# A two-layer graph network on one core: node states and destination rows kept in SBUF instead of DRAM, and a reordered end

## The reference

```python
h = relu(layernorm(x))                      # layer 0: GATv2
xl, xr = h @ Wl + bl, h @ Wr + br
m = leaky_relu(xl[src] + xr[dst] + edge_weight1 @ We, 0.2)
p = softmax of (m @ att) over the edges of each dst
g = gelu(h + segment_sum(xl[src] * p, dst) + bias_out)
x = x + batchnorm(g) * bn_gamma + bn_beta
h = relu(layernorm(x))                      # layer 1: gated messages
em = relu(layernorm(concat(h[src], h[dst]) @ msg_w + msg_b)) * edge_weight
messages = segment_sum(em, dst) / counts
gate = sigmoid(h @ gate_w + gate_b)
u = relu(layernorm(concat(h, messages) @ upd_w + upd_b, upd_g, upd_beta))
x = x + gate * u + (1 - gate) * h
```

## Time and profile before

| | |
|---|---|
| median of 3 runs | 2326.95 us (2321.8 to 2328.92) |
| the profiled execution | 2325.57 us, span 2323.7 us |
| busy share of the span | PE 69%, PEld 50%, DVE 66%, ACT 44%, POOL 71% |
| granted TensorE clock, mean of the span | 0.921 of full speed |
| DMA | 233.58 MB in 222657 packets, mean 101 GB/s |
| costliest group | L697, GpSimd's gathers: 1638 of them, 1573.8 us busy, mean 961 ns |

### The profile page before, as it was taken

The page is one execution under the profiler, slowest core; times in us unless marked ns, Lnnn a source line. Parts: engine busy times, 40 slices in busy tenths (PEclk is TensorE's granted clock), DMA queues, the critical chain, the costliest instruction groups (busy, mean ns, idle before and its releaser), DMA issues.

```text
span 2323.7 us, 45075 instructions
## 1 busy us (share of the span) xinstructions
PE 1608.6 (69%) x10064; PEld 1151.3 (50%) x10064; DVE 1539.4 (66%) x5042; ACT 1027.0 (44%) x3827; POOL 1646.2 (71%) x1729
## 2 busy tenths in 40 slices
PE   5588787777777777777676776656566656656564
PEld 4366454555545555555465554444444444445443
DVE  6667665656565555655568886776666667676757
ACT  4444443444444444434454554444444444444435
POOL 5677777777777777777037777777777777777753
PEclk9799999999999999999778898998989899898997
DMA  8633333333333333333652343333333333333324
GB/s 222 181 99 98 96 96 88 96 89 95 88 96 92 93 95 88 95 88 77 158 166 70 98 106 96 87 95 87 95 87 94 91 91 86 93 96 88 93 63 111
DMA packets 222657, 233.58 MB, mean 101 GB/s; under 512 B 116266, under 2 KB 166332, under 8 KB 222533
## 3 DMA queue, kind: packets, MB, share of 16 engines
q0 software_dynamic: 55168, 114.83, 20.1%
q1 hardware_dynamic: 165958, 117.37, 18.8%
q10 hardware_dynamic: 1472, 0.73, 0.2%
HBM read 196.29 MB, written 36.46 MB: 100 GB/s over the span
## 4 chain that ended last, share of the span: by engine, by line
POOL 53%; issue 20%; PE 11%; DVE 7%; DMA 6%; ACT 1%; POOLq 1%; SPq 1%; DVEq 0%; ACTq 0%
POOL room L697 53%; DMA room<-src_table,rec 3%; PE psum L951 2%; PE psum L878 2%; PE psum L956 1%; PE psum L969 1%; DMA dst_table<-rows 1%; PE psum L778 1%; PE psum L860 1%; PE psum L850 1%; PE psum L843 1%; DMA room<-state 1%; DVE stats L1352 1%; DVE rows L1364 0%; PE psum L868 0%
## 5 line engine op out<-in xcount | busy, mean ns | idle before, releaser
L697 POOL DMA_INDIRECT room<-src_table,rec x1638 | 1573.8, 961 | 523.8 <-issue 486.1
L951 PE MATMUL psum<-room,ident 128*128 128x384 f32 (+1 forms) x512 | 273.1, 619 | 370.5 <-DMA room<-src_table,rec 313.9
L1242 ACT ACTIVATE room<-psum 128x128 f32<-128x128 f32 x832 | 219.0, 274 | 541.4 <-DVE room L1778 538.8
L1592 DVE TENSOR_TENSOR room<-psum,room 128x384 f32<-128x384 f32 (+1 forms) x256 | 151.2, 591 | 386.9 <-ACT room L1174 216.3
L1174 ACT ACTIVATE room<-psum 128x384 f32<-128x384 f32 (+1 forms) x256 | 131.8, 515 | 523.2 <-PE psum L850 516.9
L1778 DVE TENSOR_TENSOR room<-psum,msg_g 128x384 f32<-128x384 f32 (+1 forms) x256 | 151.0, 590 | 275.9 <-PE psum L956 267.6
L951 PEld LDWEIGHTS psum<-room,ident 128*128 128x128 f32 x512 | 85.7, 210 | 404.0 <-issue 363.7
L969 PE MATMUL psum<-room 128*125 128x128 f32 x1664 | 264.4, 302 | 1.6 <-ACT room L1254 1.6
L878 PE MATMUL psum<-room 128*125 128x128 f32 x1664 | 254.0, 293 | 16.5 <-ACT room L1192 10.6
L956 PEld LDWEIGHTS psum<-room 125*128 125x128 bf16 x2496 | 185.9, 108 | 129.5 <-issue 107.5
L1792 DVE SCALAR_TENSOR_TENSOR room<-room,rstd_e,msg_beta 128x128 f32<-128x128 f32 x832 | 242.5, 349 | 10.2
(11 more groups left out here) (224 smaller groups left out, 2228.6 us busy)
## 6 DMA issues: line engine op xcount, KB each, us to landing
room<-dst_perm SPq DMA_DIRECT2D x128, 416.0 KB
room<-src_table,rec POOLq DMA_INDIRECT x1638
room<-dst_table SPq DMA_DIRECT2D x128, 64.0 KB
src_table<-rows SPq DMA_DIRECT2D x24, 224.0 KB
dst_table<-rows SPq DMA_DIRECT2D x24, 224.0 KB
st_in<-state SPq DMA_DIRECT2D x64, 65.5 KB
st_in<-state SPq DMA_DIRECT2D x64, 64.0 KB
state<-st_out SPq DMA_DIRECT2D x64, 64.0 KB
```

Of the source, the lines that this page charges most:

```text
L697: pool.indirect_dma_start(out=xg[:, u, t * P:(t + 1) * P], out_offset=None, in_=table[:, :], in_offset=bass.IndirectOffsetOnAxis(ap=rec[:, ...
L951: nc.tensor.matmul(msg_bank[b][:, cols], ident[:, :], xg[:, u, t0 * P:t1 * P], start=True, stop=False, skip_group_check=True)
L1242: i = nc.scalar.activation(sq[:, j * P:(j + 1) * P], msg_bank[b][:, j * P:(j + 1) * P], ACT.Square, accum_out=var_e[:, c, j:j + 1])
```

## The change

Every state stays in SBUF. `held` is [125 partitions, 52 tiles, 128], `held_den`, `held_max` and `cnt` hold sum, maximum and count, and `dst_rows` holds the destination rows; all are filled where they are made, and nothing of them passes through DRAM. For this the layout is turned: node n is on partition n % 125, in tile n // 125. A window of 125 nodes that starts anywhere then lies on all 125 partitions, in two neighbouring tiles: partitions from `left` up belong to tile `start`, those below to `start` + 1. The pair's entry in `pair_list` holds chunk, `start`, `base` and `left`. VectorE reads `start` into a register twice per pair (`start_of`), makes two columns `side` (1 where the partition belongs to the first or the second tile), picks the window's rows (`pick_rows`), and merges into both tiles, with factors that are neutral where `side` is 0. SyncE's window, state and factor loads and the state stores are gone; the load of the pair's entry now waits for the state of pair k-2. The masks of layer 0 are bf16 instead of f32. `feat_h` and `held` share one room, which is zeroed by GpSimd in two fills behind the projections and by VectorE before the second loop.

Between the loops, TensorE turns `node_h` in place of the product with `feat_h`. At the end, the update weights and bias are centred over the features ahead of time, so that the product's rows have mean zero: the statistics then are a sum of squares by ScalarE (`squares_out`). The product `upd_beta` x gate is made for 10 groups by GpSimd and 3 groups by ScalarE, to be added by VectorE: `weighted` (one pass per group), `gated` (one per tile), `added` (one per group). `OUT_PARTS` has five parts. `GB_ACT` is (10, 11, 12).

The core of the diff, with the indent cut by 8; most of the removed lines are left out, since they stand above:

```diff
+feat_room = sb("feat_room", [P, NC * D])
+feat_h = feat_room[:, 0:NT * PP].rearrange("p (t n) -> p t n", n=PP)
+held = feat_room[0:PP, :].rearrange("p (t f) -> p t f", f=D)
+dst_rows = sb("dst_rows", [PP, NC, D])
+cnt = sb("cnt", [PP, NC])
+held_den = sb("held_den", [PP, NC])
+held_max = sb("held_max", [PP, NC])
...
-nmask = take(2 * CH).rearrange("p (u e) -> p u e", u=2)
+nmask = take(CH).bitcast(BF16).rearrange("p (u e) -> p u e", u=2)
...
-    return table[0:N, :].rearrange("(p t) f -> p t f", t=NT)[p0:p1, t0:t1, :]
+    return table[0:N, :].rearrange("(t p) f -> p t f", p=PP)[p0:p1, t0:t1, :]
...
+            if not there(k, -2, end):
+                return
+            two, three = two_chunks(k + 2)
...
+            sp.wait_ge(s.oh, k + 1)
+            settle(sp)
+            if n == 0:
+                sp.wait_ge(s.mask, nth(k + 1, 0))
                 settle(sp)
-                sp.wait_ge(s.split, k + 1)
+            load_dst(s, v, two)
+            if n == 0:
...
+                load_ew(two, v)
+            ge(sp, s.state, k - 1)
+            settle(sp)
+            load_info(s, k + 2, (u + 2) % U)
+        all_pairs(sp, slot, last, 0)
...
+    done = 10 * GT * PP
+    pool.wait_ge(s_proj, 10)
+    pool.memset(feat_room[:, 0:done], 0.0).then_inc(s_zero, 1)
+    pool.wait_ge(s_proj, NG)
+    pool.memset(feat_room[:, done:NC * D], 0.0).then_inc(s_zero, 1)
...
-    for g in RELU_POOL:
-        pool.wait_ge(s_ub, g + 1)
+    pool.wait_ge(s_gate, NG)
+    pool.wait_ge(msg.win, last + U)
+    for g in GB_POOL:
         for t in range(*GROUPS[g]):
-            i = pool.tensor_scalar(msum[0:PP, t, :], msum[0:PP, t, :], gate[:, t:t + 1], 0.0, ALU.mult, ALU.max)
...
+            i = pool.tensor_scalar(gb[:, t, :], upd_beta[0:PP, :], gate[:, t:t + 1], None, ALU.mult)
+        i.then_inc(s_gb_pool, 1)
...
         for t in range(t0, t1):
...
+            nc.tensor.matmul(turn_ps[g % 2][:, t - t0, 0:PP], node_h[:, t, :], ident[0:PP, 0:PP],
+                             start=(t == t0), stop=False, is_transpose=True, skip_group_check=True)
+        pe.wait_ge(s_att, g + 1)
+        for t in range(t0, t1):
+            i = nc.tensor.matmul(turn_ps[g % 2][:, t - t0, 0:PP], held[:, t, :], ident[0:PP, 0:PP],
...
+    for g in (2, 3):
         own_in_bank(g)
+    pe.wait_ge(msg.hg, nth(last + U, 0))
+    pe.wait_ge(msg.sq, nth(last + U, 0))
+    for g in (0, 1):
+        own_in_bank(g)
+    pe.wait_ge(msg.state, last + U)
     turn_msg(0)
+    turn_msg(1)
+    for g in (4, 5):
+        own_in_bank(g)
     for g in range(NG):
...
             lagged(gat_prob, k, u, b, 6, end)
+            lagged(gat_exp, k, u, b, 4, end)
             if b == 0 and there(k, -1, end):
                 split_high(gat, k + 1, (u + 1) % U)
-            if b == 2 and there(k, -1, end):
+            if b == 1 and there(k, -1, end):
                 split_mid(gat, k + 1, (u + 1) % U)
-            lagged(gat_exp, k, u, b, 4, end)
...
-    def norm_out(g):
-        t0, t1 = GROUPS[g]
-        act.wait_ge(s_norm_scale, PART0[2] + part_of(2, g) + 1)
+    def offsets(g):
+        for t in range(*GROUPS[g]):
+            i = nc.scalar.activation(gb[:, t, :], upd_beta[0:PP, :], ACT.Copy, scale=gate[:, t:t + 1])
+        i.then_inc(s_gb_act, 1)
+    def squares_out(g):
+        t0, t1 = GROUPS[g]
+        act.wait_ge(s_zg, g + 1)
...
         for t in range(t0, t1):
...
+            i = nc.scalar.activation(sqz[0:PP, g % 2, t - t0, :], z_bank(g)[:, t - t0, :], ACT.Square, accum_out=ln_a[:, t:t + 1])
+        i.then_inc(s_zq, 1)
+    def deviations_out(p):
...
+        act.wait_ge(s_zq, g1)
...
+    act.wait_ge(msg.win, last + U)
+    for g in GB_ACT:
+        offsets(g)
+    AHEAD = 2
+    for g in range(AHEAD):
         msg_features(g)
...
     for p, (g0, g1) in enumerate(OUT_PARTS):
         for g in range(g0, g1):
...
+            if g + AHEAD < NG:
+                msg_features(g + AHEAD)
+            squares_out(g)
+        deviations_out(p)
...
+    for i, w in enumerate((upd_w[:, 0:D], upd_m[:, :], upd_b[:, :])):
+        k = dve.tensor_reduce(wmean[:, i:i + 1], w, AX_X, ALU.add)
+    link(k)
+    link(dve.tensor_scalar(wmean[:, 0:3], wmean[:, 0:3], 1.0 / D, None, ALU.mult))
+    for i, w in enumerate((upd_w[:, 0:D], upd_m[:, :], upd_b[:, :])):
+        link(dve.tensor_scalar(w, w, wmean[:, i:i + 1], None, ALU.subtract))
+    dve.drain().then_inc(s_updc, 1)
...
+    def starts_of(slots):
+        settle(dve)
+        _, found = nc.values_load_multi_w_load_instructions(
+            slots, engines=[dve.engine], min_val=0, max_val=NT,
+            skip_runtime_bounds_check_because="the list is built within these bounds")
+        return found
+    def start_of(u):
+        return starts_of(pair_info[0:1, u, 1:2])[0]
+    def nodes_of(s, k, u):
+        v = u % 2
+        base, left = (pair_info[:, u, i:i + 1].bitcast(F32) for i in (2, 3))
+        dve.wait_ge(s.dst[v], turns(s, k, v, 2, 32, last))
+        dve.tensor_scalar(side[:, u, 0:1], iota_p[:, :], left, None, ALU.is_ge)
+        dve.tensor_scalar(side[:, u, 1:2], iota_p[:, :], left, None, ALU.is_lt).then_inc(s.side, 1)
+        dve.wait_ge(s.side, k + 1)
+        dve.tensor_scalar(turned[:, :], side[:, u, 1:2], float(W), base, ALU.mult, ALU.add).then_inc(s.turned, 1)
+        if s is gat:
+            dve.tensor_scalar(far[:, u, :], side[:, u, :], -FAR, FAR, ALU.mult, ALU.add)
+        dve.wait_ge(s.turned, k + 1)
+        dve.tensor_tensor(node_id[:, v:v + 1], turned[:, :], iota_p[:, :], ALU.add).then_inc(s.id, 1)
+    def pick_rows(s, k, u, start):
+        v = u % 2
+        rows_of = [dst_rows[:, bass.ds(start + j, 1), :].rearrange("p a f -> p (a f)") for j in range(2)]
+        dve.tensor_scalar(dfar[0:W, :], rows_of[1], side[0:W, u, 1:2], None, ALU.mult).then_inc(s.far, 1)
+        dve.wait_ge(s.far, k + 1)
+        settle(dve)
+        dve.scalar_tensor_tensor(out=dwin[0:W, v, :], in0=rows_of[0], scalar=side[0:W, u, 0:1], in1=dfar[0:W, :],
+                                 op0=ALU.mult, op1=ALU.add).then_inc(s.win, 1)
...
+    def gat_merge(k, u, start):
...
         dve.wait_ge(s.nloc, k + 1)
         ge(dve, s.esh, k)
         settle(dve)
...
+        dve.tensor_scalar(nloc2[0:W, :], far[0:W, u, :], nloc[0:W, u:u + 1], None, ALU.add).then_inc(s.near, 1)
+        dve.wait_ge(s.near, k + 1)
...
+        dve.tensor_tensor(newmax[0:W, :], held_max[:, at], nloc2[0:W, :], ALU.min).then_inc(s.nnew, 1)
         dve.wait_ge(s.nnew, k + 1)
...
+        dve.tensor_tensor(shift[0:W, 0:2], newmax[0:W, :], held_max[:, at], ALU.subtract)
+        dve.tensor_tensor(shift[0:W, 2:4], newmax[0:W, :], nloc2[0:W, :], ALU.subtract).then_inc(s.sh, 1)
+        dve.scalar_tensor_tensor(out=cnt[:, at], in0=side[0:W, u, :], scalar=cloc[0:W, u:u + 1], in1=cnt[:, at],
+                                 op0=ALU.mult, op1=ALU.add)
+        dve.wait_ge(s.sh, k + 1)
...
+        dve.tensor_copy(held_max[:, at], newmax[0:W, :])
+    def gat_add(k, u, start):
...
+        for j in range(2):
+            i = dve.tensor_scalar(part[0:W, j, :], sum_bank[v][0:W, 0:D], eshift[0:W, 2 + j:3 + j], None, ALU.mult)
+        i.then_inc(s.part, 1)
...
+        dve.tensor_scalar(den2[0:W, :], eshift[0:W, 2:4], den[0:W, v:v + 1], None, ALU.mult)
+        dve.tensor_tensor(old2[0:W, :], held_den[:, at], eshift[0:W, 0:2], ALU.mult).then_inc(s.old, 1)
...
+        dve.tensor_tensor(held_den[:, at], den2[0:W, :], old2[0:W, :], ALU.add)
+        for j in range(2):
+            rows_j = held[:, bass.ds(start + j, 1), :].rearrange("p a f -> p (a f)")
+            dve.scalar_tensor_tensor(out=rows_j, in0=rows_j, scalar=eshift[0:W, j:j + 1], in1=part[0:W, j, :],
+                                     op0=ALU.mult, op1=ALU.add)
...
+        now = (u - 2) % U
...
+            if b == 0 and there(k, -1, end):
+                nodes_of(gat, k + 1, (u + 1) % U)
+                pick_rows(gat, k + 1, (u + 1) % U, start_of((u + 1) % U))
             if b == 1 and there(k, 2, end):
-                gat_merge(k - 2, (u - 2) % U)
+                start = start_of(now)
+                gat_merge(k - 2, now, start)
             if there(k, -1, end):
                 if b == 1:
                     split_rest(gat, k + 1, (u + 1) % U)
                     one_hot(gat, k + 1, (u + 1) % U)
+                if b == 2:
+                    split_low(gat, k + 1, (u + 1) % U)
                 if b >= 2:
...
-                if b == 3:
-                    split_low(gat, k + 1, (u + 1) % U)
             if b == 2 and there(k, 2, end):
-                gat_add(k - 2, (u - 2) % U)
+                gat_add(k - 2, now, start)
...
+    def msg_nodes(k, u):
...
+        base, left = (pair_info[:, u, i:i + 1].bitcast(F32) for i in (2, 3))
+        dve.tensor_scalar(wrap[:, :], iota_w[:, :], left, float(W), ALU.is_lt, ALU.mult).then_inc(s.wrap, 1)
+        dve.wait_ge(s.wrap, k + 1)
```

(56 more changed lines are left out.)

461 lines of the change are left out of this document (160 added, 301 removed).

## The result

| | before | after |
|---|---|---|
| median | 2327.39 us (4 runs, 2321.8 to 2328.92) | 2288.49 us (4 runs, 2284.79 to 2292.73) |
| ratio | | 0.983, 95% interval 0.9816 to 0.9845 |
| profiled execution, span | 2323.7 us | 2283.7 us |
| VectorE busy, GpSimd busy | 66%, 71% | 78%, 72% |

The account below looks back on a forecast made before the run. GpSimd's row gathers were taken to bound both loops, so time could be won only outside them: -4 + 0 + 4 - 13 - 15.5 = -28.5 us, forecast 2298 us, 8-in-10 range 2280 to 2345.

Parts of the forecast that it names:

- Loops at the gathers' pace: Both loops: VectorE takes 15.2 us a pair (14.4 to 16.8), below the gathers' 16.3, so time changes by 0.
- My rival: Second loop: VectorE decides from 15.66 us a pair; 15.7 to 16.1 gives about 2313 us (0.12), beyond 16.1 0.17.
- below 16.3: Both loops: VectorE's pairs under 16.3 us leave the loops at the gathers' pace.
- the last number of that sum, -1.2: First loop, VectorE per pair: the last term of 14.7 + 3.9 - 2.2 - 1.2 = 15.2 us.
- Gathers beside a busier VectorE: Both loops: VectorE's added passes slow each gather by 0.0025 us, +4 us in all; bounds 0 and +0.02 each.
- The third rival: Both loops: VectorE's traffic slows gathers by 0.02 us each, giving 2327 us; chance 0.05.
- Opening: Before the first table gather: fewer store waits against new steps and fills, net -4 us, between -9 and +3.
- Between the loops: Last gather of the first loop to next table gather: no state store and reload, -13 us, bounds -17 and -8.
- The 2 us set aside for TensorE's clock: Between the loops: TensorE at the lower of its two clocks could take back 2 us of the gain.
- End: After the last gather: earlier VectorE start (-4.5 us) and shorter passes, -15.5 us in all, bounds -19 and -9.
- What would show it: Signs across the profile: gather spacing, first table gather, the two gaps, VectorE's second-loop share, and the chain on L697.

Follow-up runs that it names:

- The first experiment: Two more 125-column VectorE passes per pair in the second loop, against the changed kernel: 2309.84 us (one run; kernel before on the same chip 2323.79).
- the four loops of the table: Loops that fetch instructions: first loop of the kernel before with 20 empty VectorE waits per pair (2333.17 us), both of the changed kernel, first with VectorE's queue shortened (1.0161, slow chip).

## Why the prediction was right, and where it was not

**Loops at the gathers' pace.** Right in result, close to wrong in fact. VectorE's pairs follow each other 15.24 us apart while it catches up (first blocks at 1277.38 and 1338.32, four pairs), where I had 15.2. That the two agree is luck: it consists of 14.3 us of work with its small gaps (13.0 of them busy) and 0.9 of waiting for TensorE, not of 15.2 of work. Its terms: a register read takes 0.30 us, not 0.6, and 0.43 us of idle before `pick_rows` go with it; a mask gained 86 ns, not 200. The wait for TensorE, which I had as filled, is still there. And 13 of the 63 distances are 18 us, by the stop at the turn, which I did not have, so the mean is 15.73. My rival put the point of decision at 15.66. VectorE's last addition comes 10.1 us behind the last gather, 10.5 before: the edge itself. The first experiment shows that there is no margin behind it. The measured threshold is the rival's (start plus 64 pairs), not the "below 16.3" of the forecast's own step: a rate below the gathers' is not enough if the engine starts 47.65 us behind them (37.0 before; the fill of 5.6 us and the new steps are the difference). In the first loop the term was too high: while VectorE catches up, the pairs there are 13.8 to 14.8 us apart, and 16.0 to 16.4 at the turns, where I had 15.2 for all; the last number of that sum, -1.2, has no source in the text or in a run.

**Gathers beside a busier VectorE.** Wrong in sign for the first loop: -4.4 instead of +2. The step looked at the added 128-column passes only. What it left out is that the change takes away the passes that did slow the gathers, the masks in f32: the earlier trace rows had them with 384 columns written in f32, and the bf16 masks alone give 5.7 us. The added passes themselves cost about what I took: with the masks alone in bf16 the 819 gathers of the first loop take 778.06 us, in the changed kernel 779.44 (up to 781.93 in its other traces). In the second loop they take 790.70 us against 789.92 before, and 793.46 with the two more passes of the first experiment; the +1.6 is 0.8 of this and 0.8 of waits. The third rival (+0.02 us each) is out.

**Opening.** -2.8 for -4. The row stores' waits went as said, but the fills cost 2.4 us where I took 2, and from run to run the opening moves by more than what is left.

**Between the loops.** -18.5 for -13. VectorE's rows:

```profile
1107.19 0.61 DVE L1646 SCALAR_TENSOR_TENSOR feat_room<-feat_room,eshift,part 125x128 f32 x2
1108.04 0.19 DVE L1699 TENSOR_SCALAR factor<-held_den 125x52 f32<-125x52 f32 x1 [0.23 <-DVEq L1648]
...
1125.93 0.83 DVE L1709 BATCH_NORM_AGGREGATE bn_mv<-bn_st 128x2 f32<-128x150 f32 x1
```

From the last gather: the last addition ends 14.0 us later (16.1 before), the first factor step 0.2 behind it (5.3 before, the store and reload), the aggregate 17.9 behind that (27.2 before, where each piece had its own factor steps and loads), and 59.4 to the next gather (61.4). I had the aggregate at 35 us behind the last gather, it is at 32.2: additions 0.9 earlier, the 13 groups a little shorter, and no 1.2 us of start. The 2 us set aside for TensorE's clock weren't needed, and the row stores gave 2.1 instead of 1.5. The mechanism was right; every reserve in it was too large, 5.5 us in all.

**End.** -15.8 for -15.5, and each term holds: start 17.3 us behind the last gather against 22.1, so -4.7 (forecast -4.5), then 34.9 us (forecast 35.4). How the -4.7 parts into order and reload, the sum did not say.

**What would show it.** Gathers 1.25 to 1.27 apart, first table gather at 62 to 66, 92 us between, 56 at the end, VectorE's share in the second loop about 85%: measured 1.256 and 1.273 over the whole loops, 65.06, 91.5, 55.9, and 490.33/600 = 82%. But the chain, which was to stay on L641's gathers (L697 before), left them in the second loop.

## What to carry to other kernels

Where one engine paces a loop, a slower neighbour shows nothing until it is at the edge: compare start + pairs x mean distance of both, turns of the loop included, not their busy shares. Take an end stage apart by its first and last row on the engine that ends it: here order and passes gave 14 of 15.8 us, the transfer that went only about 2. And a change that adds work beside a pacing engine may also take away the work that was slowing it, so look at which forms lie beside its slow instructions.

## What the runs showed of the hardware

- A VectorE TENSOR_SCALAR step of 13 columns took 3.79 us under GpSimd's fills of 5000 and 1656 columns (4.28 and 1.50 us) and ended with them; it took 0.17 without them. Steps of the same size with two inputs took 0.17 under the same fill. The Trainium skill (GPSIMD Engine Reference, Specifications) says that the two share their SBUF interfaces, with contention for VectorE instructions in a two-port mode or with two SBUF inputs. The trace agrees on the sharing, in the direction from GpSimd to VectorE; its steps with two inputs (L1320, L1321) were not held by a fill.
- Beside masks written in f32 from int16 48 of 101 gathers took over 0.96 us; with this part alone in bf16 it was 15 of 92, though the pass got shorter by only 96 ns (431 to 335), and the loop 5.7 us shorter.
- A register read of SBUF by VectorE takes 0.30 us (256 of them, 299 to 318 ns); one of DRAM by SyncE about 1.05 us (242, median 1053 ns).
- A loop's instructions are fetched anew in each turn (five packets of about 8 KB), or never. Where they are, the next queue entry comes 3.0 to 4.3 us behind the branch entry, in every turn of the four loops of the table; where they are not, 0.3 to 0.4.
